# Fused decoder layer on one core: other rank offsets for the halves of a batch row, and other look-aheads, in the planner that writes the engines' orders

## The reference: what is computed

```
# 1: a Mamba block and a SwiGLU MLP
u, z   = split(rmsnorm(x) @ in_proj.T)             # 2 x 1024 features
u      = silu(conv4(u));  dt, B, C = x_proj(u)     # dt = softplus(...)
h[t]   = exp(dt[t]*A) * h[t-1] + dt[t]*B[t]*u[t]   # 1024 channels x 16 states, t in order
y      = (sum_n h[t,n]*C[t,n] + u*D) * silu(z)
h1     = x + y @ out_proj.T
x      = layernorm(x + h1 + (silu(n(h1) @ w1.T) * (n(h1) @ w2.T)) @ w3.T)   # n = rmsnorm, 2048 wide
# 2: cross attention on 64 keys, 16 heads; each head's temperature comes from
#    statistics (mean, max, entropy) over all 1024 queries of the batch row
x      = layernorm(x + softmax(q @ k.T / (2*t)) @ v @ Wo.T)
# 3: dense layer plus a rank-16 correction, top 2 of 8 experts
x      = layernorm(x + x @ W.T + b + lora(x))
```

## Time and profile before

| | |
|---|---|
| median of 3 runs | 4376.36 us |
| profiled execution, its own time | 4379.0 us |
| its span | 4377.2 us |
| granted TensorE clock, mean | 0.901 of full speed |
| PE busy | 3725.6 us, 85% of the span |
| PEld (weight loads) busy | 1749.1 us, 40% |
| DVE / ACT / POOL busy | 2522.7 / 2161.6 / 2488.3 us |
| DMA, over the span | 483.17 MB, mean 110 GB/s |

### The profile page before, as it was taken

The page is one execution under the profiler, slowest core; times in us unless marked ns, Lnnn a source line. Parts: engine busy times, 40 slices in busy tenths (PEclk is TensorE's granted clock), DMA queues, the critical chain, the costliest instruction groups (busy, mean ns, idle before and its releaser), DMA issues.

```text
span 4377.2 us, 36093 instructions
## 1 busy us (share of the span) xinstructions
PE 3725.6 (85%) x9848; PEld 1749.1 (40%) x9848; DVE 2522.7 (58%) x3319; ACT 2161.6 (49%) x5177; POOL 2488.3 (57%) x1100
## 2 busy tenths in 40 slices
PE   6555999799979988899999998899998988899677
PEld 3111434343334334544344334534444333544344
DVE  2665478657756883367735885267744886122211
ACT  3443454565465454556526555466526554443344
POOL 0998399649954993079914994059932996000000
PEclk9555999899989998899999998899999998899788
DMA  4333344334523541144423442134423442112000
GB/s 147 115 113 101 104 155 156 111 120 154 164 95 113 164 157 59 63 140 144 152 86 111 155 153 77 63 121 147 146 84 103 160 154 89 40 57 67 25 21 28
DMA packets 221267, 483.17 MB, mean 110 GB/s; under 512 B 31884, under 2 KB 32268, under 8 KB 220812
## 3 DMA queue, kind: packets, MB, share of 16 engines
q1 hardware_dynamic: 221068, 480.87, 34.3%
HBM read 470.82 MB, written 9.96 MB: 110 GB/s over the span
## 4 chain that ended last, share of the span: by engine, by line
PE 54%; POOL 16%; DVE 12%; issue 8%; ACT 8%; DMA 1%; SPq 0%; POOLq 0%; DVEq 0%; ACTq 0%
PE ps L1490 28%; POOL hb L961 10%; DVE hb L1296 6%; POOL hb L951 6%; PE ps L1579 5%; PE ps L1548 5%; PE ps L1591 5%; PE ps L1658 1%; PE ps L1624 1%; PE ps L1603 1%; PE ps L1541 1%; PE ps L1518 1%; ACT ps L1171 1%; PE ps L1670 1%; PE ps L1559 1%
## 5 line engine op out<-in xcount | busy, mean ns | idle before, releaser
L951 POOL TENSOR_TENSOR hb<-dtu,bc 128x1024 f32<-128x1024 f32 x512 | 1205.6, 2356 | 73.3 <-PE ps L1591 31.0
L961 POOL TENSOR_TENSOR hb<-hb,bc 128x1024 f32<-128x1024 f32 x512 | 1205.6, 2355 | 60.7 <-ACT state L1086 35.4
L1490 PE MATMUL ps<-fT,wden 128*128 128x512 f32 x2304 | 1053.6, 607 | 28.6 <-DVE hm L1334 21.1
L1010 ACT ACTIVATE ps<-dt,a_neg 128x512 f32<-128x512 f32 x1024 | 690.9, 688 | 693.3 <-DVE hb L1296 690.2
L1591 PE MATMUL ps<-hb,ident 128*128 128x512 f32 x1024 | 632.4, 706 | 306.3 <-POOL hb L961 303.4
L1490 PEld LDWEIGHTS ps<-fT,wden 128*128 128x128 f32 x2304 | 444.2, 195 | 597.2 <-issue 596.4
L1296 DVE TENSOR_TENSOR_SCAN hb<-ps,state,hb 128x512 f32<-128x512 f32 x512 | 626.7, 1266 | 14.1 <-ACT ps L1010 7.2
L1296 DVE TENSOR_TENSOR_SCAN hb<-ps,hb 128x512 f32<-128x512 f32 x512 | 596.2, 1206 | 21.1 <-POOL hb L951 13.4
L1305 DVE TENSOR_TENSOR ps<-ps,hb 128x512 f32<-128x512 f32 x512 | 355.5, 694 | 364.8 <-POOL hb L961 363.9
L1579 PE MATMUL ps<-wden,hm 128*128 128x512 f32 x1024 | 487.7, 623 | 17.5 <-DVE res L1350 12.8
L1490 PE MATMUL ps<-xnT,wmix 128*128 128x512 f32 x1024 | 468.6, 609 | 12.8 <-ACT xnT L1034 8.7
(11 more groups left out here) (192 smaller groups left out, 3894.4 us busy)
## 6 DMA issues: line engine op xcount, KB each, us to landing
bc<-bc_dram SPq DMA_DIRECT2D x1024, 256.0 KB, 3.7
wden<-in_w SPq DMA_DIRECT2D x192, 512.0 KB, 3.7
wmix<-in_w_mix SPq DMA_DIRECT2D x96, 512.0 KB, 3.6
watt<-in_w_qof SPq DMA_DIRECT2D x32, 512.0 KB, 4.3
xm<-in_x SPq DMA_DIRECT2D x8, 1024.0 KB, 5.5
res<-in_x SPq DMA_DIRECT2D x8, 1024.0 KB, 5.6
wden<-in_w_qof SPq DMA_DIRECT2D x16, 512.0 KB, 3.8
out<-res SPq DMA_DIRECT2D x8, 1024.0 KB, 4.3
```

Source lines behind the costliest of these rows:

```text
L951: TTn(hb[:, k % 4], dtu[:, :, :], bc[:, 0, k % 3].unsqueeze(1).broadcast_to([P, 2, CH]), ALU.mult).then_inc(s.s1_ready, 1)
L961: TTn(hb[:, k % 4], hb[:, k % 4], bc[:, 1, k % 3].unsqueeze(1).broadcast_to([P, 2, CH]), ALU.mult).then_inc(s.s3_done, 1)
L1010: A_(dst, dt[:, p % 2, jj], ACT.Exp, scale=a_neg[:, j, n:n + 1]).then_inc(full_of(key), 1)
L1490: ins = M(dst, a, b, start=start and n == 0, stop=stop and n == len(pairs) - 1)
```

## The change: what it does

```diff
--- before.py
+++ after.py
@@ -331,7 +331,7 @@
 
 RING_F, DENSE_BANKS = (0, 1, 2, 3), (4, 5, 6, 7)
 WORK = {"x": 176.0, "s": 103.0, "y": 304.0}
-PHASE = {"y": 6.0, "s": 7.0, "x": 8.0}
+PHASE = {"y": (6.12, 6.26), "s": (7.49, 7.0), "x": (9.46, 7.8)}
 
 
 def y_weights():
@@ -397,7 +397,7 @@
             pending.add(u)
             share[name] = share.get(name, {})
             share[name][u[1]] = share[name].get(u[1], 0.0) + sum(p[1] for p in got)
-            key = 0 if name == "m" else 1 if name == "l" else u[1] + PHASE[name] + share[name][u[1]] / WORK[name]
+            key = 0 if name == "m" else 1 if name == "l" else u[1] + PHASE[name][u[1] % 2] + share[name][u[1]] / WORK[name]
             by_eng = {}
             for n, p in enumerate(got):
                 by_eng.setdefault(p[0], []).append((n, p))
@@ -483,7 +483,7 @@
     return streams["m"], begun, {u: v[0] for u, v in done.items()}, order, taken
 
 
-LOOK = {"m": 0.3, "l": 0.3, "x": 0.3, "y": 0.3, "s": 0.3}
+LOOK = {"m": 0.25, "l": 0.1, "x": 0.09, "y": 0.3, "s": 0.3}
 MIXER, BEGUN, DONE, ORDER, DENSE_TAKES = schedule()
 
 
```

## The result

The changed kernel takes 4235.83 us (median of 4 runs, 4232.14 to 4238.94) against 4376.11 us: the ratio is 0.9676, 95% interval 0.966 to 0.9693. The forecast was 4238. The profiled execution has a span of 4234.6 us, 142.6 less than before.

A forecast was written before the change was run, and what follows sets the result against it. The mixer was taken as held while PE works off x and y lists, with POOL pacing scans. Holds -246, scans +101 and +8, fronts +24, tail -25: -138, so 4241 profiled, 4238 median; 8 in 10: 4175 to 4335.

The forecast's parts named there:

- holds: POOL's stretches without work between a scan and `ht`, chunks 3 to 7: 330 us instead of 576, -246.
- fronts: Stretches of about 67 us between `ht` and the next scan: +24 for both behind chunks 3 and 5, others the same.
- scans: Mixer's scans, paced by POOL: 3, 5, 7 to 355 us each at PE's 0.93, +101; 4 and 6 together +8.
- Rival D: Odd holds don't give, as `ht` still waits for queries and x(1); only even holds shrink: 4383 us, chance 0.05.
- Rival A: More room in the scans: they stay on POOL's line, 0.3 us for each us of dense work: 4190, chance 0.15.
- Rival B: PE's work is conserved: hold time returns in scans, only 58 us of PE's idle time saved: 4318, chance 0.16.
- Rival C: Scans 3, 5, 7 lose 1.4 us per step to late ACT, 269 us instead of 101: 4406, chance 0.06.
- Tail: Dense work behind the last `turn_out`: 373.8 us instead of 405.5, as half of x(5) comes earlier: -25.

The follow-up runs named there:

- e8: Kernel before the change, with 12 matmuls of each chunk's dense layer (base) left out on PE: 4304.25 us, ratio 0.9844.
- e3: Changed kernel, with the end of x(c-3) (router, rank units, base, norm, store) forced behind `out` of chunk c: 4431.99 us, ratio 1.0135.
- e11: Changed kernel, with the planner's costs set as measured and other PHASE and LOOK tables: 4197.77 us, ratio 0.958.
- e7: Changed kernel, orders kept, with 12 matmuls of each chunk's dense layer (base) left out on PE: 4173.57 us, ratio 0.9545.
- e5: Changed kernel, attention exponentials as one instruction for four heads, without heads' biases, scales and sums, `den` set once: 4221.7 us, ratio 0.9655.
- e9: Changed kernel, with 12 residual adds (L1433) in scans 3, 5, 7 moved behind the scan step they preceded on DVE: 4236.95 us, ratio 0.9666.
- e10: Changed kernel, with the norm's reciprocal (L1257) moved behind the next scan step on DVE, in all seven scans: 4235.14 us, ratio 0.9665.
- e1: Changed kernel's offsets (PHASE) alone, with LOOK at 0.3 for every list: 4347.16 us, ratio 0.9946.
- e2: Changed kernel's look-aheads (LOOK) alone, with the old PHASE (6, 7, 8 for both halves): 4335.64 us, ratio 0.9922.

## Why the prediction was right, and where it wasn't

**The time** was right to 2 us, and the direction of each big term too. That it is as close as 2 us is luck, since errors cancel. The holds alone are 108 us shorter than forecast and the fronts 107 longer, which is one border put in the wrong place. Beside that, against the forecast the scans came 24 us shorter, scan 3 started 11 us earlier, holds and fronts behind 3 to 6 are 31 us longer (567 against 536), and from the last scan's end on it is 609 against 608.

**Holds.** That PE's list between `out` and `turn_in` sets the time in which the mixer stands still is shown by e8 (10 us less in the list, 7 to 13 less in the hold) and by e3 (holds where the list put them). One reading was loose: the 518 us that PE is busy in the five holds aren't all dense work, `out` is 137 of them. The split was wrong. I let all of that list count before L982. In the changed kernel `ht` needs only `out`, the residual and these two instructions of x(1) on DVE (L1426, L1429), so POOL goes on 50 us after the scan, and the rest of the list is counted in the front, 64 and 61 us longer than before where I had 12. Rival D, which kept the odd holds, is out by the holds, though most of it lives on in the fronts of 131.1 and 128.6.

**Scans.** The size was right for scans 3 and 5 (354 for 355) and 16 us too long for scan 7 (339), and the step behind it holds only in part. I priced the odd scans by PE's rate, 0.93 over the scan. The trace has PE at 0.955 in the first 258 us of scan 5 and at 0.85 in the last 97, so 0.93 is a mean and not a pace. What the runs show in its place: the length doesn't follow from the amount of work (e3, and e11's scan 3), and with x close together the mixer's steps wait for x's chain in each in-order list, 29 us in six waits. PE is still part of it. It is full from 2585 to 2614, and in e7 its missing work comes off scan and hold in full. The wait of 6.70 us is held by DVE's add and by ACT's exponentials, each long enough alone (e5 and e9), and that of 6.10 by the reciprocal (e10). That of 5.22 stands by PE's order behind the router, which no run took away. For the other three it is open, and so is what time all six are worth, since no run shortened the scans by freeing one.

**Rival A** (scans near 339) is right for scan 7, and e11 shows the room that it spoke of: up to 224 us of dense work cost no more than 0.3 us for each (27 more in scan 4 cost 4), where x is spread. Spreading was not varied by itself, as e11 changes all the tables. The weight loads' share, for which I cited the Trainium skill's "Perfetto Trace Analysis", section "Identifying the Most-Contended Engine", was the better reading of that: it is 0.44 in e11's scan 4 (148 of 333 us) where it was 0.42 before. I put the odd scans by the rule at 331, which no row gives: scan 5 has 157 us of weight loads, and at hold 4's share (39.25 of 86) they make some 344, an estimate. The scans are 354; the share tells what PE could take, not what the other lists let it. **Rival B** (all work comes back) is refuted: PE's idle time fell by 96 us and its busy time by 47. **Rival C**, ACT late by 1.4 us in each step, isn't there: POOL's waits for ACT went from 35.4 to 30.5 us, and the scans are 85 us longer, not 269. ACT is late at single places, though (e9's row of 5.18 us).

**Tail.** Forecast -25, measured +9 from the hold's end and -80 with the hold (-81 forecast): the same shift of the border as in the odd fronts.

**What the change does** is not told by its name. e1 and e2 show that offsets and look-aheads bring 0.5% and 0.8% apart. The offsets alone leave the ends of x(0), x(2), x(4) behind `out` in full; the look-aheads alone empty only the even holds and make the scans longer. And x's end ahead of `out`, on which the prediction built the shorter holds, is one way and not the only one: e11 keeps it behind `out` at chunks 3, 5 and 7 and gains 1% more.

## What to carry to other kernels

Where an engine with a fixed pace alternates with stretches in which it stands still, count what the fullest engine's list holds in each of the two, and price the two separately. Then look at how it lies within the paced stretch: 212 us of dense work stood beside a scan of 321 us where x was spread (e11, scan 3), and 209 and 212 us beside scans of 341 and 368 where x came as one chain towards the end (e3). A share over a whole stretch can be right by averaging two regimes, so cut it once more before building on it; and when a wait has two late inputs, removing one leaves the time as it was and doesn't clear that input.

## What the runs showed of the hardware

Two things were not expected. With the same matmuls PE's recorded busy time moved from 3725.6 to 3678.8 us with the granted clock (0.901 to 0.911), so busy time compares work between two orders only to a per cent or so. And an L1205 of 64 columns costs ACT 0.38 us from start to start, its read of the sum within that; one instruction for 256 columns without bias, scale by head and sum (e5) took 0.36 to 0.37 from start to start. Yet some 19 us less of ACT's busy time for each of 8 chunks (2173.1 to 2022.9 us in all) took only 7 us off the span of the changed kernel and 21 off that of the kernel before.
